# Row maxima of the second attention layer added by a selector matmul instead of DMA-written stack rows

## The reference

```python
q = jnp.einsum('bsd,hdk->bhsk', Q, Wq) + bq[None, :, None, :]
k = jnp.einsum('bsd,hdk->bhsk', K, Wk) + bk[None, :, None, :]
v = jnp.einsum('bsd,hdk->bhsk', V, Wv) + bv[None, :, None, :]
scores = jnp.einsum('bhqk,bhsk->bhqs', q, k) * scale
attn = jax.nn.softmax(scores, axis=-1)
ctx = jnp.einsum('bhqs,bhsk->bhqk', attn, v)
```

## Time and profile before

| | |
|---|---|
| median of three runs | 300.1 us |
| span of the profiled execution | 296.9 us |
| mean granted TensorE clock | 0.839 of full |
| TensorE busy, matmul / weight load | 209.6 / 154.6 us |
| VectorE busy | 198.1 us |
| ScalarE busy | 118.0 us |
| GpSimd busy | 83.7 us |

### The profile page before, as it was taken

The page is one execution under the profiler, slowest core; times in us unless marked ns, Lnnn a source line. Parts: engine busy times, 40 slices in busy tenths (PEclk is TensorE's granted clock), DMA queues, the critical chain, the costliest instruction groups (busy, mean ns, idle before and its releaser), DMA issues.

```text
span 296.9 us, 4777 instructions
## 1 busy us (share of the span) xinstructions
PE 209.6 (71%) x1541; PEld 154.6 (52%) x1541; DVE 198.1 (67%) x561; ACT 118.0 (40%) x273; POOL 83.7 (28%) x110
## 2 busy tenths in 40 slices
PE   2723674555987868767887787777976979572996
PEld 1422553343655747535566565554765756251684
DVE  4656866246886786678876976678578764915673
ACT  2500664603587363305683452153552612061221
POOL 1402676134436131315281312150412011000000
PEclk9955699555599999995899999967799889779699
DMA  3553612102101220030002200200020002000000
GB/s 110 185 144 99 235 46 67 49 2 59 33 3 25 62 64 13 11 97 0 2 15 58 70 18 0 67 5 4 7 51 0 0 2 53 20 2 2 0 0 18
DMA packets 21895, 12.61 MB, mean 42 GB/s; under 512 B 2966, under 2 KB 20998, under 8 KB 21878
## 3 DMA queue, kind: packets, MB, share of 16 engines
q1 hardware_dynamic: 20790, 11.88, 14.7%
q10 hardware_dynamic: 1088, 0.52, 0.7%
HBM read 5.44 MB, written 0.54 MB: 20 GB/s over the span
## 4 chain that ended last, share of the span: by engine, by line
PE 33%; DVE 27%; issue 15%; POOL 7%; ACT 6%; DMA 5%; SPq 5%; DVEq 0%; POOLq 0%; ACTq 0%
PE bank L1130 5%; PE bank L1085 4%; PE bank L1150 4%; DVE mx L743 3%; DVE xn L721 3%; POOL rstd L375 3%; ACT pt L554 3%; PE bank L1071 3%; POOL es L416 2%; DVE ct L762 2%; SPq L258 2%; SPq L261 2%; PE bank L1102 2%; DVE es L733 2%; PE bank L1039 2%
## 5 line engine op out<-in xcount | busy, mean ns | idle before, releaser
L416 POOL TENSOR_TENSOR es<-es,mx 128x512 f32<-128x512 f32 x32 | 33.4, 1055 | 37.9 <-DVE mx L728 36.8
L542 ACT ACTIVATE es<-es 128x512 f32<-128x512 f32 x32 | 19.1, 625 | 33.9 <-POOL es L416 33.8
L1060 PE MATMUL bank<-ident,es 128*128 128x128 f32 x128 | 25.4, 346 | 9.9 <-ACT es L542 9.7
L375 POOL TENSOR_TENSOR rstd<-ve,half 128x2 f32<-128x2 f32 x16 | 11.2, 699 | 73.8 <-DVE ve L715 73.4
L593 ACT ACTIVATE gth<-bank 128x256 f32<-128x256 f32 (+1 forms) x36 | 13.2, 380 | 34.1 <-PE bank L1130 34.0
L733 DVE TENSOR_TENSOR es<-bank,biasq 128x512 f32<-128x512 f32 x32 | 21.2, 684 | 7.8 <-PE bank L1044 7.7
L1060 PEld LDWEIGHTS bank<-ident,es 128*128 128x128 f32 x128 | 19.0, 178 | 14.1 <-ACT es L542 13.7
L1130 PE MATMUL bank<-xnT,wg 128*128 128x256 f32 (+1 forms) x72 | 25.6, 439 | 0.6 <-DVE gb L858 0.4
L852 DVE SCALAR_TENSOR_TENSOR ga<-gth,bank 128x256 f32<-128x256 f32 (+1 forms) x36 | 15.0, 416 | 15.0 <-ACT gth L593 14.9
L1085 PE MATMUL bank<-pt,va 128*32 128x128 f32 x512 | 24.8, 290 | 0.0
L1130 PE MATMUL bank<-xnT,wu 128*128 128x256 f32 (+1 forms) x72 | 22.9, 403 | 0.0
(11 more groups left out here) (132 smaller groups left out, 408.8 us busy)
## 6 DMA issues: line engine op xcount, KB each, us to landing
kst<-ksp SPq DMA_DIRECT2D x24, 64.0 KB, 2.6
qst<-qsp SPq DMA_DIRECT2D x48, 32.0 KB
kst<-ksp SPq DMA_DIRECT2D x48, 32.0 KB
qst<-qsp SPq DMA_DIRECT2D x24, 64.0 KB, 2.5
biasq<-rel_bias_scratch SPq DMA_DIRECT2D x2, 512.0 KB, 4.6
wg<-in_wg SPq DMA_DIRECT2D x1, 544.0 KB, 4.1
wu<-in_wu SPq DMA_DIRECT2D x1, 544.0 KB, 5.6
wd<-in_wd SPq DMA_DIRECT2D x1, 512.0 KB, 5.7
```

Of the source, the lines that this page charges most:

```text
L375: pool.tensor_tensor(rstd[:, n, :], ve[:, n, :], half[:, 0:2], ALU.pow).then_inc(sem(f"rstd{n}"), 1)
L416: pool.tensor_tensor(es[:, b, h], es[:, b, h], mx[:, 0, b, h].unsqueeze(2).broadcast_to([128, 4, SEQ]), ALU.subtract).then_inc(sem(f"less0 ...
L542: act.activation(es[:, b, h], es[:, b, h], ACT.Exp, scale=-1.0).then_inc(sem(f"p0{b}"), 1)
L1060: ins = pe.transpose(dst[:, s * SEQ:(s + 1) * SEQ], es[:, b, 4 * c + s], ident[:])
```

## The change

The ones, their DMAs, the six extra rows of both stacks and the DMAs of `max_rows` are gone. A 0/1 array `maxsel` of 48 rows by 16 heads by 128 columns comes in as an input and is loaded in the setup (192 KB). For head s of a tile it selects, from the 48 rows of `nmT`, the three parts of that head's maximum, and spreads them over all 128 key rows. In `scores1_turned` four score matmuls of 96 rows open a tile, and four matmuls of 48 rows with `maxsel` as weights and `nmT` as the moving side add the maxima to the same bank.

```diff
-MROWS = SROWS + 6
-        qst = [sb("qst0", [SROWS, HALF, 2, TOK], BF16), sb("qst1", [MROWS, HALF, TOK], BF16)]
-        kst = [sb("kst0", [SROWS, HALF, TOK], BF16), sb("kst1", [MROWS, HALF, 2, TOK], BF16)]
+        qst = [sb("qst0", [SROWS, HALF, 2, TOK], BF16), sb("qst1", [SROWS, HALF, TOK], BF16)]
+        kst = [sb("kst0", [SROWS, HALF, TOK], BF16), sb("kst1", [SROWS, HALF, 2, TOK], BF16)]
-        ones = sb("ones", [3, HALF, TOK], BF16)
+        maxsel = sb("maxsel", [3 * HEADS, HEADS, SEQ], U16)
-            def max_rows(b, turn):
-                freed(sp, "m", f"nmT1{b}", turn)
-                sp.dma_start(qst[1][SROWS:MROWS, :, b * SEQ:(b + 1) * SEQ],
-                             nmT[:, b, :]).then_inc(sem(f"max1{b}_in"), 16)
-            sp.wait_ge(sem("ones"), 1)
-            for hh in range(2):
-                r = SROWS + 3 * hh
-                sp.dma_start(kst[1][r:r + 3, :, hh, :], ones[:]).then_inc(sem("kst_ones"), 16)
+            sp.dma_start(maxsel[:], maxsel_d).then_inc(sem("maxsel_in"), 16)
-                    max_rows(0, i)
-                    max_rows(1, i)
-            max_rows(0, "tail")
-            max_rows(1, "tail")
-            dve.memset(ones[:], 1.0).then_inc(sem("ones"), 1)
             def scores1_turned(b, p, turn):
 
-                after(pe, f"max1{b}_in", p, of=16)
+                freed(pe, "m", f"nmT1{b}", turn)
                 for c in range(4):
                     dst = fill(pe, "t", f"T1{b}{c}", turn)
                     tok = slice(b * SEQ, (b + 1) * SEQ)
                     for s in range(4):
                         hp, hh = 2 * c + s // 2, s % 2
-                        ins = pe.matmul(dst[:, s * SEQ:(s + 1) * SEQ], kst[1][:, hp, hh, tok],
-                                        qst[1][:, hp, tok], start=True, stop=True)
+                        pe.matmul(dst[:, s * SEQ:(s + 1) * SEQ], kst[1][:, hp, hh, tok], qst[1][:, hp, tok],
+                                  start=(s == 0), stop=False, skip_group_check=True)
+                    for s in range(4):
+                        ins = pe.matmul(dst[:, s * SEQ:(s + 1) * SEQ], maxsel[:, 4 * c + s].bitcast(BF16), nmT[:, b],
+                                        start=False, stop=True, skip_group_check=True)
                     filled(ins, "t", f"T1{b}{c}", turn)
-            pe.wait_ge(sem("kst_ones"), 32)
+            pe.wait_ge(sem("maxsel_in"), 16)
+def max_selector():
+
+    out = np.zeros((2, 3, HALF, HALF, 2, SEQ), np.uint16)
+    for hp in range(HALF):
+        for hh in range(2):
+            out[hh, :, hp, hp, hh] = 0x3F80
+    return out.reshape(3 * HEADS, HEADS, SEQ)
```

More of the change, by code:

```diff
@@ L10 @@
 U8 = mybir.dt.uint8
+U16 = mybir.dt.uint16
 ACT = mybir.ActivationFunctionType
@@ L37 @@
 SROWS = 2 * HROWS
-MROWS = SROWS + 6
 VW = 32
 def bass_xattn_ffn_moe(nc, x_d, ctx_d, mask_d, wqk_d, wv_d, wo_d, bqk_d, bv_d, rows_d, table_d, u1t_d, v1_d, b1_d,
-                       u2t_d, v2_d, gate_d, wg_d, wu_d, wd_d, swd_d, ident_d, onehot_d, expsel_d, out_d):
+                       u2t_d, v2_d, gate_d, wg_d, wu_d, wd_d, swd_d, ident_d, onehot_d, expsel_d, maxsel_d, out_d):
     rel_d = nc.dram_tensor("rel_bias_scratch", (HEADS, REL + 1), F32, kind="Internal").ap()
@@ L1371 @@
         "expsel": expert_selector(),
+        "maxsel": max_selector(),
     }
```

## The result

The changed kernel takes 307.8 us (median of four runs, 306.4 to 309.4) against 300.1 us (299.9 to 301.5): 1.023 times the kernel before, 95% interval 1.018 to 1.028. Repeated later on another chip, it was 1.024 (1.018 to 1.030). The forecast of 303.2 us had the direction and less than half of the size, and the time lies outside the range of 299.8 to 305.8.

A forecast was written before the change was run, and what follows sets the result against it. The prediction took a dependency chain, not an engine, as the bound. Body(1) and body(2) +1.8, body(3) +1.5 and tail -0.2 us gave +3.1 and 303.2 us; own range 301.8 to 304.6, over all 299.8 to 305.8.

The forecast's parts named there:

- the setup changes: Setup: two DMAs of the ones become one of 192 KB, their memset goes; 0 us, at most 1.8 either way.
- no slack: Behind T11 in the bodies: the delay passes from the contexts down the whole chain to the next body.
- What a selector matmul costs: Score tiles: selectors start 0.056 us apart at full clock, 0.104 at half; four add 0.22 or 0.42 us a tile.
- the forecast's sum: Growth of the eight groups: 0.44 us each at full clock; body(3) T10 +1.0, its T11 +0.5.
- Rival (d): Selectors cost the upper bound, 0.11 us apart; full-clock groups cost about 1.0, not 0.44: 306.0 us; chance 0.04.
- the bounds: Selector spacing: 0.043 us from 32-column matmuls below, 0.11 from f32 transposes above; 0.17 or 0.44 us a tile.
- the 81 ns a pair: Skill page's rate for weight load and matmul pairs with 128 columns; would make the estimate 1 us higher, 304.2.
- the forecast's +3.1: Whole kernel: body(1) and body(2) 1.8 us, body(3) 1.5, tail -0.2, added to the profiled execution's 296.9.
- the removal: Tail without the maxima's DMA: T10 starts 1.2 us sooner, T11 0.7 sooner; nothing gained in six of eight groups.
- Rival (b): T10 of body(3) and tail: more matmuls keep or restore full clock; 298.6 us, one stretch alone 300.5 to 301.3; chance 0.14.
- Rival (c): All four groups of body(1) and body(2) fall to half clock, costing 1.0 not 0.44 each: 305.4 us; chance 0.12.
- 3.2 us around the span: Outside the profiled span: 3.2 us from 296.9 to the median of 300.1, left unchanged.

The follow-up runs named there:

- nosel: Changed kernel with the selector matmuls left out, so the maxima are not taken away: 297.0 us (seven runs), ratio 0.989 to the kernel before.
- pad96: Changed kernel with selector and turned maxima padded with zero rows from 48 to 96: 301.2 us (twelve runs), ratio 1.0027 to the kernel before.
- pad64: Changed kernel with selector and turned maxima padded with zero rows from 48 to 64: 307.0 us (one run).
- pad65: Changed kernel with selector and turned maxima padded with zero rows from 48 to 65: 301.7 us (one run).
- switch4: Changed kernel with selectors before scores in every second tile, four switches a group instead of eight: 309.0 us (four runs), ratio 1.027; again 307.5 us (six runs), 1.023.

## Why the prediction was wrong

**What was right.** That the DMA is hidden in all bodies and waited for in the tail only: nosel shows body groups of unchanged length and start. That both tail waits go (T10 starts 1.2 us sooner behind the scores, T11 0.7 behind the values). That the setup changes give nothing visible: nosel has them too and starts T10 of body(1) at 85.97, before at 85.96. That the added matmuls are on the chain: in body(2), at equal clock, T11 starts 4.73 us behind T10 where it was 3.81.

That this delay passes to the end is right too, but the sums fit better than they should. The groups of the bodies grow by four times 0.83, 0.62 and 2.0, which is 5.9 us, and the last store is 5.6 us later. In the changed kernel's execution, though, T11 of body(1) starts 6.30 us behind T10, because what lies between them, L1031 and the values of T10, fell to half clock. Timeline of the changed kernel, then the windows of that stretch before and after:

```profile
88.92 2.79 PE L1075 MATMUL bank<-pt,va 128*32 128x128 f32 x32
```

```profile
88.50:91.50 3.00, 2.44 (x47) 1.90 (x44) 3.00 (x6) 1.96 (x6) 1.80 (x2) 1.00 0.03 5
```

```profile
88.50:91.50 3.00, 3.00 (x37) 2.29 (x35) 2.90 (x5) 0.86 (x3) 1.39 (x2) 0.50 0.02 5
```

In the second profiled execution of the same kernel (after_again) it is 4.74 us there, so this one stretch cost 1.6. Another, from 187 to 191 us, cost 1.5. Against them stand 1.9 us in the later part of body(3), where before had two stretches at half clock and the changed kernel none, 0.6 by which body(1) started sooner, and 0.5 in each of body(1) and body(2): from the contexts of T11 to the output projection it takes 1.85 us in place of 2.37, so a part of the delay was absorbed where the forecast saw no slack. (Before, VectorE's L768 took 0.90 us there while GpSimd's L406 ran beside it, now 0.46 with it over; whether the one causes the other was not tried.) That these terms nearly cancel is luck. The size of the effect rests on the runs (7.7 us by the medians, 1.8 to 2.8%), not on this sum.

**The step that failed: "What a selector matmul costs".** The forecast took 0.22 us for four selectors at full clock from a stream of equal matmuls. A selector itself does cost that: 0.057 apart within a block, and pad96, which has the added work without the switch, has full-clock groups of 2.41 us against 2.39 forecast. Its eight groups together grew by 4.9 us, which is the forecast's sum. What was missing is a term of its own, which the forecast put at nothing: two switches a tile at 0.11 us, eight a group. At half clock, where TensorE is the bound, the seven inside a group show in full (4.39 us against 3.62 in pad96, 0.77 more). At full clock they show by half (2.78 against 2.41), because pad96 still waits for ScalarE, 0.24 us ahead of its third tile for one, and the hold-ups fill such waits. The eight groups, before and after:

| group | before, us | after, us | grew | forecast |
|---|---|---|---|---|
| body(1), body(2), four groups | 1.95 to 1.97 | 2.77 to 2.80 | 0.83 each | 0.44 each |
| body(3) T10, half clock | 2.40 | 4.40 | 2.0 | 1.0 |
| body(3) T11 | 2.18 | 2.80 | 0.6 | 0.5 |
| tail T10, half clock | 2.39 | 4.41 | 2.0 | 1.2 |
| tail T11, part at half clock | 1.97 | 3.42 | 1.5 | 0.44 |

The sum of the growth is 9.4 us against 4.9 forecast. Of the 4.5 between them, the four full-clock groups of body(1) and body(2) give 1.6 and the two at half clock 1.8, nearly all of it the switches (0.2 of T10 in body(3) is the forecast's own: without switches it grew by 1.2 in pad96, not 1.0); 0.1 is T11 of body(3), and 1.0 is T11 of the tail, where switches and a first half at half clock add up.

**Rival (d)** priced a selector at 0.11 us apart and so came to the right size of a full-clock tile (0.44) by a wrong mechanism; it had a chance of 0.04, and it added nothing for the groups at half clock. Its 0.11 was itself divided wrongly: eight transposes have seven distances, and (1.09-0.2)/7 is 0.13. The range ended at 305.8 because the bounds were sought among streams of one kind of matmul, none of which has a switch in it.

**It could have been read.** The trace of before has a switch of just this kind, 48-row matmuls followed by 128-row ones, and beside it the same place with 96 rows. Timeline of TensorE, body(1):

```profile
83.44 0.39 PE L1039 MATMUL bank<-kst,qst 96*128 96x256 bf16 x2 [0.20 <-DVE mx L743]
83.67 0.60 PE L1015 MATMUL bank<-xcT_sb,wqk 128*128 128x256 f32 x2
...
111.70 0.39 PE L1144 MATMUL bank<-combT_sb,expsel 48*128 48x256 bf16 x2 [1.05 <-ACT combT_sb L584]
112.02 0.70 PE L1130 MATMUL bank<-xnT,wg 128*128 128x256 f32 x2
```

Both pairs are bf16 with 256 columns and are followed by f32. Behind the 96-row pair the next matmul starts 0.23 us after the first of the pair, behind the 48-row pair 0.32 us after it: 0.09 more, with the type and the columns alike. The Trainium skill has a rule too, page "TensorEngine Tiling (Array Packing)", section "Key Properties": changing the tiling mode drains TensorE. By the Trainium skill's section "Available Configurations" on that page the modes have 128, 64 or 32 rows. pad64 and pad65 agree with such a step at 64 rows, at 0.11 us a change; the price stands in the traces alone. What the forecast weighed instead, the 81 ns a pair of the Trainium skill's page "TensorE: Matmul & The Clock Gate", section "Back-to-back issue gap", gives the right mean for a tile of eight (0.65/8 = 0.081) but not what happens: 0.055 within a block and 0.11 more at the borders, and 0.055 throughout once the switch is gone.

**What stays open.** The switches explain the groups, but not every microsecond of the runs. With them gone the forecast's +3.1 should have come out; pad96 is 2.6 us above before by the spans of single executions, 1.6 by the medians, and by the ratio of the runs 0.8, at most 1.8. A part of that may be the removal, forecast at 1.2 and 0.7 us in the tail and measured at about 3 by the runs of nosel, of which its trace shows 1.7. And the switch4 kernel kept its time with shorter groups.

The granted clock moves such sums: the two profiled executions of the changed kernel had spans of 304.6 us at 0.835 and 307.9 us at 0.811, and in the second the T11 of the tail ran wholly at half clock. Rival (b) did not come: T10 of body(3) and of the tail stayed at half clock. Rival (c) did not come as priced, since all four groups of body(1) and body(2) kept full clock in both executions; but it priced the groups alone, and the stretch behind T10 of body(1) shows what the values cost when they fall. That the change shifts the clock on the whole is not shown: the mean was 0.836 over nine runs of the changed kernel and 0.839 over 45 of the kernel before. The forecast also took 3.2 us around the span. It is 1.8 in every run for which both are known (306.4 less 304.6): the profiled execution of before was itself quicker than the median. This moves nothing in the difference.

## What to carry to other kernels

A matmul added to a stream costs its columns and also the borders it makes: look up in the trace what happens between unlike matmuls, not only how far apart like ones are. Here padding a 48-row operand with zeros to 65 or 96 rows was faster than leaving it small, and alternating small and large matmuls one by one was far slower than blocks of four. And a DMA whose wait shows up only in the tail is not worth replacing by work that every loop body pays for.

## What the runs showed of the hardware

- A switch of matmuls between up to 64 rows and over 64 rows held TensorE up by 0.11 us, at full and at half clock alike (blocks of four 0.33 against 0.22, 0.54 against 0.43). At full clock the first matmul behind a border starts 0.15 us after the one ahead of it and the next one 0.067, in place of 0.056 each. 48 or 64 rows against 96 cost this, 65 against 96 does not. Nor does 102 against 96: before, the last 102-row matmul of T10 in body(1) starts at 87.70 and the first 96-row one of L1044 at 87.76.
- A gap of 0.09 us stands in nosel between 96-row scores and the values, whose weights are 32 columns wide in f32: the last of the eight matmuls from 87.76 starts at 88.16, and the values start at 88.30, 0.15 later in place of 0.056. No experiment was made of it, but neither the rows (96 to 128) nor the type makes a gap at 83.67 above. The width of the weights alone does in the trace of the changed kernel, where f32 matmuls of 128 rows follow one another, once with 128 and once with 64 columns of weights ahead of L1140. The step is 0.43 us in the first case and 0.53 in the second:

```profile
251.40 0.59 PE L1120 MATMUL bank<-xnT,wu 128*128 128x256 f32 x2
251.83 0.61 PE L1140 MATMUL bank<-wd,hT 128*128 128x128 f32 x4
...
254.78 0.59 PE L1120 MATMUL bank<-xnT,wu 128*64 128x256 f32 x2
255.31 0.71 PE L1140 MATMUL bank<-wd,hT 128*128 128x128 f32 x4
```

- Adding to a bank costs no more than overwriting it (0.31 to 0.33 us a block either way).
